# A decoder on one core: two multiplications of the delta layer computed by GpSimd in place of VectorE

## What is computed

```python
beta = jax.nn.sigmoid(b)
g = -jnp.exp(A_log) * jax.nn.softplus(a + dt_bias)
def step(S, xs):
    qt, kt, vt, gt, bt = xs
    S = S * jnp.exp(gt)[..., None, None]
    kv = jnp.einsum('bhk,bhkv->bhv', kt, S)
    delta = (vt - kv) * bt[..., None]
    S = S + jnp.einsum('bhk,bhv->bhkv', kt, delta)
    o = jnp.einsum('bhk,bhkv->bhv', qt * scale, S)
    return (S, o)
...
xf = o.astype(jnp.float32) * jax.nn.silu(z.astype(jnp.float32))
var = jnp.mean(xf * xf, -1, keepdims=True)
xn = xf * jax.lax.rsqrt(var + NORM_EPS) * norm_weight
return xn.reshape(B, T, VALUE_DIM) @ w_out.T
```

## Time and profile before

| | |
|---|---|
| Three runs | 2426.64, 2412.61 and 2424.78 us, median 2424.78 |
| Profiled execution | span 2424.5 us; the page gives no other time of it |
| PE busy | 2112.7 us, 87% |
| VectorE busy | 1856.6 us, 77% |
| ScalarE busy | 1477.2 us, 61% |
| GpSimd busy | 216.2 us, 9% |
| Mean granted TensorE clock | 0.931 of full speed |

### The profile page before, as it was taken

The page is one execution under the profiler, slowest core; times in us unless marked ns, Lnnn a source line. Parts: engine busy times, 40 slices in busy tenths (PEclk is TensorE's granted clock), DMA queues, the critical chain, the costliest instruction groups (busy, mean ns, idle before and its releaser), DMA issues. The chain is left out here.

```text
span 2424.5 us, 42274 instructions
## 1 busy us (share of the span) xinstructions
PE 2112.7 (87%) x16920; PEld 1596.5 (66%) x16920; DVE 1856.6 (77%) x3341; ACT 1477.2 (61%) x2466; POOL 216.2 (9%) x163
## 2 busy tenths in 40 slices
PE   7997447999999999999986589899999996888855
PEld 4666325777777777878774345788888873555633
DVE  4776667888989898889867834478888776678697
ACT  3664255667777777776736631577777775455365
POOL 0000100000100010101100042000000000100313
PEclk8998768999999999999988799999999996999977
DMA  3000012222222221222116355311010000200001
GB/s 159 2 1 12 13 34 53 72 83 57 64 56 66 56 64 54 62 74 80 36 49 212 129 143 176 115 32 57 23 27 6 5 18 1 81 2 1 16 1 35
DMA packets 164785, 135.14 MB, mean 56 GB/s; under 512 B 118512, under 2 KB 145776, under 8 KB 157936
## 3 DMA queue, kind: packets, MB, share of 16 engines
q1 hardware_dynamic: 160752, 126.02, 16.6%
q0 software_dynamic: 3840, 6.43, 1.4%
HBM read 106.42 MB, written 25.98 MB: 55 GB/s over the span
## 5 line engine op out<-in xcount | busy, mean ns | idle before, releaser
L1593 DVE SCALAR_TENSOR_TENSOR ctx_chan<-l1a_raw,l1a_cw,ctx_chan 128x1024 f32<-128x1024 f32 x192 | 232.0, 1279 | 3.5 <-issue 3.5
L1200 PE MATMUL banks<-x_chan,l1a_wp 128*128 128x512 f32 x512 | 225.2, 598 | 4.8 <-ACT l1a_vt L1488 4.8
L1200 PEld LDWEIGHTS banks<-x_chan,l1a_wp 128*128 128x128 f32 x512 | 98.0, 192 | 122.6 <-issue 116.7
L3166 PE MATMUL banks<-x_chan,more_weights_ahead 128*128 128x128 f32 x1024 | 123.6, 275 | 1.2 <-ACT l2a_kT L2693 1.2
L3166 PEld LDWEIGHTS banks<-x_chan,more_weights_ahead 128*128 128x128 f32 x1024 | 121.6, 192 | 3.9 <-ACT l2a_kT L2693 2.0
L1187 POOL TENSOR_TENSOR l1a_al<-l1a_aT,l1a_outer 128x1024 f32<-128x1024 f32 x32 | 75.0, 2364 | 483.2 <-DVE l1a_aT L1653 483.2
L1237 PE MATMUL banks<-l1a_wo,l1a_oT 128*128 128x256 f32 x512 | 117.7, 383 | 0.0
L2706 ACT ACTIVATE l2a_masked<-l2a_masked,l2a_rowmax 128x128 f32<-128x128 f32 x256 | 99.0, 392 | 28.9 <-DVE l2a_rowmax L2919 28.9
L3202 PE MATMUL banks<-l2a_wo,l2a_oT 128*128 128x256 f32 x512 | 114.5, 382 | 0.0
L1208 PE MATMUL banks<-l1a_wz,x_chan 128*128 128x256 f32 x512 | 113.4, 380 | 0.0
L3202 PEld LDWEIGHTS banks<-l2a_wo,l2a_oT 128*128 128x128 f32 x512 | 96.2, 190 | 14.3 <-issue 1.0
(11 more groups left out here) (648 smaller groups left out, 5644.1 us busy)
## 6 DMA issues: line engine op xcount, KB each, us to landing
l1a_sq<-l1a_norm_mem SPq DMA_DIRECT2D x16, 1024.0 KB, 4.7
ctx_tok<-l1a_rows_mem SPq DMA_DIRECT2D x16, 1024.0 KB, 8.1
l1f_wgu<-in_l1f_wgu_dram SPq DMA_DIRECT2D x4, 1408.0 KB, 11.4
moe_sums<-l1x_zero SPq DMA_DIRECT2D x2, 2176.0 KB, 18.3
ctx_chan<-in_ctxT_dram SPq DMA_DIRECT2D x2, 2048.0 KB, 13.8
l1a_wp<-in_l1a_wp_dram SPq DMA_DIRECT2D x8, 512.0 KB, 5.5
l1f_wgu<-moe_sums SPq DMA_DIRECT2D x8, 512.0 KB, 7.5
x_chan<-in_xT_dram SPq DMA_DIRECT2D x4, 512.0 KB, 5.2
```

Source lines behind the costliest of these rows:

```text
L1200: mm = MM(projected(i, u)[:, q * 512:(q + 1) * 512], wp[:, c, u * 128:(u + 1) * 128], g.xT[:, c, t0:t0 + 512], start=c == 0, stop=c == 1)
L1593: V.scalar_tensor_tensor(t, raw[:, u, :, j:j + S], cw[:, c, j:j + 1], t, ALU.mult, ALU.add).then_inc(s["conv_done" if step == 2 else "conv ...
L3166: mm = mm_(ps[:, 4 + q % 2, k * 128:(k + 1) * 128], wq[:, c, SHARE * q + k, :], g.xT[:, c, tile(i)], start=c == 0, stop=c == 1)
```

## The change

`weigh` and `scale_gated` are taken out of VectorE's stream and written into GpSimd's. The operands, the formulas and the semaphores that they raise (`e_made`, `normed`) stay the same. In GpSimd's stream the order of a round is now: two multiplications by the outer mask, the two scalings of the round before, the two weighings for the next round, and in every second round the scaling of the output weights. The weighing of round 0 waits in addition for the gates (`gates_made`). The last round's gated values, which are scaled after the loop (L1830), stay on VectorE.

```diff
+            def weigh(i, h):
+                k, b0 = i // 2, batch0(i) + 4 * h
+                t = heads(e, h).rearrange("p (b r) n -> p b r n", r=2)
+                pool.wait_ge(s["decay_exp"], 2 * i + h + 1)
+                P.tensor_tensor(t, t, bc(beta[:, b0:b0 + 4, 2 * k:2 * k + 2], 3, 128), ALU.mult).then_inc(s["e_made"], 1)
+
+            def scale_gated(i, h):
+                pool.wait_ge(s["g_rs"], i + 1)
+                P.tensor_tensor(heads(go, h), heads(go, h), bc(rs[:, HALF * h:HALF * h + HALF], 2, 128), ALU.mult).then_inc(s["normed"], 1)
+
             pool.wait_ge(s["rest_loaded"], 16 * 4)
             scale_out(0)
+            pool.wait_ge(s["gates_made"], 2)
+            for h in range(2):
+                weigh(0, h)
             for i in range(ROUNDS):
                 for h in range(2):
                     if i:
                         pool.wait_ge(s["r_made"], 4 * i)
                     pool.wait_ge(s["a_made"], 2 * i + h + 1)
                     P.tensor_tensor(heads(al, h), heads(aT, h), bc(outer[:], 1, HALF), ALU.mult).then_inc(s["al_made"], 1)
+                if i:
+                    for h in range(2):
+                        scale_gated(i - 1, h)
+                if i + 1 < ROUNDS:
+                    for h in range(2):
+                        weigh(i + 1, h)
                 if i % 2 == 0 and i:
                     scale_out(i // 2)
...
@@ VectorE, round_ @@
                 for h in range(2):
                     take_products(i, h, att, 1).then_inc(s["att_made"], 1)
-                if i:
-                    for h in range(2):
-                        scale_gated(i - 1, h)
                 invert(i)
...
-                if more:
-                    for h in range(2):
-                        weigh(i + 1, h)
...
@@ VectorE, before the rounds @@
                 for h in range(2):
                 scan(0, h)
-            for h in range(2):
-                weigh(0, h)
```

More of the change, by code:

```diff
@@ L1634, in normalise @@
                                        ALU.mult).then_inc(s["kq_normed"], 1)
[L1636 to L1640, removed]
             def scan(i, h):
@@ L1722, in sum_gated @@
                 V.tensor_reduce(ss[:, HALF * h:HALF * h + HALF], heads(oT, h), AX.X, ALU.add).then_inc(s["gsum"], 1)
-            def scale_gated(i, h):
-                v.wait_ge(s["g_rs"], i + 1)
-                V.tensor_tensor(heads(go, h), heads(go, h), bc(rs[:, HALF * h:HALF * h + HALF], 2, 128), ALU.mult).then_inc(s["normed"], 1)
             def add(i, h):
```

## The result

The changed kernel takes 2471.47 us, the median of 4 runs (2462.73 to 2478.21). Beside it the kernel before took 2423.9 us (2412.61 to 2426.64, 4 runs). The ratio is 1.021, with a 95% interval of 1.0184 to 1.0237: slower, by 47.6 us in the medians. The forecast was 2510 us, 38.5 us too much, with a range of 2459 to 2555. The profiled execution has a span of 2464.3 us against 2424.5, a difference of 39.8 us, and what follows accounts for that difference. The 7.8 us between it and the difference of the medians stay open: the mean granted clock was 0.931 in the profile before and 0.939 in this one, and the profiled run of the changed kernel, 2466.12 us, is the second fastest of its four.

A forecast was written before the change was run, and what follows sets the result against it. VectorE's stretch from the block inverse to the fold add was taken to bound each round. Port collisions of 5.7 us in 14 rounds (80) plus 5 for first and last gave 2424.5 + 85 = 2510 us, range 2459 to 2555.

The forecast's parts named there:

- VectorE's relief is worth nothing: Both pairs taken off VectorE are followed by idle gaps they don't cause, so removing them gains nothing.
- The hand-over of the scaled values keeps its slack: GpSimd's scalings end at 946.14, PE transposes the values from 949.60: over 3 us to spare.
- The engines shut each other out, and the weighing does it inside the taps: SBUF port collisions: two weighings among VectorE's taps, in order tap, weigh, tap, weigh; +4.7 us a round.
- The price of 2.364 us for a GpSimd multiplication: Each moved multiplication was priced like the outer-mask one of the same shape; upper bound 2.59 us.
- The held inverse, +1.3 us: GpSimd's scalings hold the block inverse on VectorE from 944.90 to 946.2, delaying scans, taps and all behind.
- Slack of 0.3 at the squares: ScalarE's squares end 0.3 us before PE needs them; taken off the 6.0 us delay, leaving +5.7 a round.
- Nothing gives the delay back: After PE's late sums the round's tail is as late as PE, so the 5.7 us stay in each round.
- First and last round, 3 and 2 us: First: no scaling, weighing beside six taps, 3 us. Last: no weighing, only the inverse held, 2 us.
- VectorE keeps the port: Weighing waits for the eighth tap, then holds fold add and last four taps; 4.2 a round, 2488 us, chance 0.24.
- The hole lowers the clock: PE idles over 5 us before the sums, its clock falls; 2 us more a round, 2538 us, chance 0.18.
- Nothing collides: Broadcast factors cause no port wait; 0 a round, at most 2 us in the last, 2427 us, chance 0.11.
- VectorE's tail was the bound: PE's back-to-back records hide that VectorE's tail bounds the round; 34 less, 2390 us, chance 0.03.

The follow-up runs named there:

- late_weigh: The changed kernel with one more wait, so that GpSimd weighs only after VectorE's last tap; 2419.29 us, ratio 1.0 to the kernel before.
- weigh_only: The changed kernel with the scalings of the gated values back on VectorE, only the weighings on GpSimd; 2465.01 us, ratio 1.0185.
- idle_pair: The kernel before plus two unused GpSimd multiplications (mask times eight beta columns) a round at the time of the weighings; 2470.26 us, ratio 1.0197.
- idle_long: The kernel before plus two unused GpSimd multiplications a round beside the taps, masked products times the mask; 2486.82 us, ratio 1.0275.
- scale_only: The changed kernel with the weighings back on VectorE, only the scalings of the gated values on GpSimd; 2419.16 us, ratio 0.9994.
- again: The changed kernel measured and profiled once more, unedited; 2466.53 us, ratio 1.0188 to the kernel before.

## Why the prediction was right, and what was mis-sized

By its own steps:

- **VectorE's relief is worth nothing**: right. *late_weigh* takes both pairs off VectorE without a held tap, at a ratio of 1.0.
- **The hand-over of the scaled values keeps its slack**: right. GpSimd has them at 966.31 + 3.75 = 970.06, 9.5 us behind the mask multiplication, and they are wanted about 13.8 us behind it.
- **The engines shut each other out, and the weighing does it inside the taps**: right, by *weigh_only*, *idle_pair* and *late_weigh*. Two taps of eight are long. The order is weigh, tap, weigh, tap, where I had a tap first, since I gave the queued tap the port after the scan.
- **The price of 2.364 us for a GpSimd multiplication**: the term that was mis-sized most. The earlier trace rows is of the same shape and engine but of the dearer pair of operands. The moved ones take 1.90, and a hold is 0.3 less than the duration, where I took almost nothing off. Held taps: 2 x 1.62 = 3.24 us measured, 4.7 forecast. Of the 1.5 us between them, 0.9 is the price and 0.6 the overlap; *idle_long* shows both apart (4.17 us with the 2.36 us kind). The lock of the quoted rule lasts for the whole instruction; the holds measured here are 0.3 us shorter.
- **The held inverse, +1.3 us**: the copy is held by 0.4 in the round shown, 0.7 in the mean (it has 801 ns in *scale_only* and 854 in the changed kernel, 176 before). What reaches the taps is 0.2 us in the round shown, 0.8 in the one before it, 0.4 in the mean of the fourteen. It failed for the same price: the scalings end 9.5 us behind the mask multiplication, where I had 10.4.
- **Slack of 0.3 at the squares**: 0.25 measured in that round, but 0.8 in the one before it and 0.55 in the mean. I read it off a single round, and one in which the block DMA landed late.
- **Nothing gives the delay back**: right; the sum of squares starts 3.1 us later and a round is 3.0 longer. In the mean of fourteen it is 0.4 + 3.25 - 0.55 = 3.1, against 1.3 + 4.7 - 0.3 = 5.7. 14 x 2.7 = 38 us too much.
- **First and last round, 3 and 2 us**: the first has its two held taps, but from the preparation to its end it is as long as before. In the last, PE is 0.7 us later at the block products behind the inverse (23.12 us behind the mask multiplication against 22.42). With differences that aren't the change's, what lies ahead of the second mask pair and behind the fourteenth round is together 2.2 us shorter, not 5 longer. Against the profiled execution the forecast is thus 38 + 5 + 2 = 45 us too high (2424.5 + 85 against 2464.3), against the median of the runs 38.5, since the profiled execution, 2466.12 us with what lies around its span, was under that median.

So the mechanism was right, and the sum about twice too large. That it stayed inside the range owes something to its width, whose lower end was built from another case (one held add a round).

The rivals. *VectorE keeps the port*: false, GpSimd went ahead even of a queued tap. *The hole lowers the clock*: it doesn't in the first profile; it does in two rounds of *again*, and is worth about 1.5 us of PE time where it happens. *Nothing collides*: false; narrow factors hold taps as others do. *VectorE's tail was the bound*: false, by *late_weigh*.

## What to carry over

Before work goes from VectorE to GpSimd, look at what VectorE runs at the moment at which the moved instruction becomes ready: if it has two SBUF inputs and its stretch is on the path, the move costs nearly GpSimd's full duration; beside PSUM-reading work it costs nothing, and in a DMA wait only what reaches beyond the wait and the slack behind it. The busy share of the relieved engine says nothing on either. Take the price of the moved instruction from a row with the same kind of operands, broadcast included; by the shape alone it was a quarter too dear here, and together with the overlap left out and a slack read off one round that made the forecast loss about twice the measured one. Read the slack from several rounds. Two moved pieces of work that need the same slack don't add up from runs with one of them each.

## What was unexpected of the hardware

- A GpSimd multiplication of 128x1024 float32 takes 1.90 us with one value per 128 neighbours or with one tile as both operands, and 2.36 us for a tile times a repeated 128x128 mask.
- The hold of a two-input multiplication is GpSimd's own duration less 0.3 us (2.05 and 2.11 for 2.36, 1.59 and 1.65 for 1.90), also for a result that nobody reads.
- A one-input GpSimd instruction holds a tap by only 0.7 us and is recorded with 3.0 to 3.6 us itself; a memset (0.95 us) holds nothing.
- A small copy of 128x8 is held like a large instruction (0.83 us instead of 0.17).
- The granted clock fell to 0.50 behind a hole of 2.2 to 4 us in some rounds and not in others of the same program.
